# A wait added to GpSimd in the first stage: it stands behind the inverse root until the batch's rows are centred

## The reference, cut to what matters

```
def apply_rope(x):
    x1, x2 = (x[..., :half], x[..., half:])
    return concatenate([x1 * cos - x2 * sin, x1 * sin + x2 * cos], axis=-1)
q = (layernorm(x) @ q_w.T + q_b)   # 16 heads of 16
k = (ctx @ k_w.T + k_b)
v = (ctx @ v_w.T + v_b)
q = apply_rope(q) * d ** (-0.5)
k = apply_rope(k)
```

## Time and profile before

| | |
|---|---|
| median of 3 runs | 4868.27 us (4863.77 to 4871.48) |
| the profiled execution's own time | 4876.46 us |
| its span in the profile | 4874.6 us |
| busy in that span | PE 93%, DVE 74%, ACT 58%, POOL 27% |
| first stage | from 0 to about 264 us of the span |
| mean granted TensorE clock of the span | 0.956 of full speed |

### The profile page before, as it was taken

The page is one execution under the profiler, slowest core; times in us unless marked ns, Lnnn a source line. Parts: engine busy times, 40 slices in busy tenths (PEclk is TensorE's granted clock), DMA queues, the critical chain, the costliest instruction groups (busy, mean ns, idle before and its releaser), DMA issues. The chain is left out here.

```text
span 4874.6 us, 82321 instructions
## 1 busy us (share of the span) xinstructions
PE 4556.2 (93%) x28528; PEld 2715.4 (56%) x28528; DVE 3620.2 (74%) x8718; ACT 2842.8 (58%) x5219; POOL 1331.2 (27%) x940
## 2 busy tenths in 40 slices
PE   8979978997699999999999999999999758999998
PEld 5546646885244444444444444444443547988897
DVE  8978865554468888888888888888886475555554
ACT  4535542223437777777777777777777213444443
POOL 7910002223620110101101101101010224666665
PEclk9989988998879999999999999999998878999999
DMA  6666653223844333343342443333321651333332
GB/s 204 197 170 189 185 154 113 87 70 123 274 94 81 50 69 73 66 82 69 57 76 57 83 80 51 69 74 66 69 49 23 184 162 33 66 83 65 64 66 38
DMA packets 248371, 471.09 MB, mean 97 GB/s; under 512 B 56584, under 2 KB 149384, under 8 KB 247936
## 3 DMA queue, kind: packets, MB, share of 16 engines
q1 hardware_dynamic: 217872, 426.43, 35.6%
q0 software_dynamic: 26720, 38.36, 4.7%
q10 hardware_dynamic: 3360, 0.98, 0.1%
HBM read 240.15 MB, written 144.94 MB: 79 GB/s over the span
## 5 line engine op out<-in xcount | busy, mean ns | idle before, releaser
L1205 DVE TENSOR_REDUCE full_peak<-full_item 128x1 f32<-128x512 f32 (+2 forms) x3392 | 2026.8, 655 | 332.2 <-PE full_item L1267 323.4
L1181 ACT ACTIVATE full_prob<-full_score 128x512 f32<-128x512 f32 (+1 forms) x3328 | 1745.7, 602 | 396.8 <-PE full_score L1277 381.2
L1267 PE MATMUL full_item<-full_kst,full_qst 49*128 49x512 f32 (+1 forms) x4096 | 1170.3, 404 | 8.4 <-DMA full_kst<-full_high 5.6
L1277 PE MATMUL full_score<-full_qst,full_kst 51*128 51x512 f32 (+1 forms) x3328 | 1021.5, 434 | 1.2 <-ACT full_prob L1181 1.2
L1267 PEld LDWEIGHTS full_item<-full_kst,full_qst 49*128 49x128 f32 x4096 | 618.8, 188 | 602.3 <-DVE full_peak L1205 538.1
L1287 PE MATMUL full_value<-full_prob,full_vaug 128*17 128x512 f32 x6656 | 884.5, 603 | 0.6 <-ACT full_prob L1181 0.4
L1277 PEld LDWEIGHTS full_score<-full_qst,full_kst 51*128 51x128 f32 (+1 forms) x3328 | 503.7, 183 | 367.8 <-ACT full_prob L1181 297.7
L1120 POOL TENSOR_TENSOR full_low<-full_low,full_keep 128x1601 f32<-128x1601 f32 x32 | 115.8, 3620 | 1997.9 <-ACT full_low L1155 1997.9
L2505 ACT ACTIVATE moe_h<-moe_hbank,moe_b 128x384 f32<-128x384 f32 (+1 forms) x320 | 199.7, 624 | 442.0 <-PE moe_hbank L2676 401.9
L2686 PE MATMUL moe_ybank<-moe_w_both,moe_h_high 128*128 128x512 f32 x1088 | 386.7, 396 | 0.0
L2539 DVE TENSOR_TENSOR moe_h_low<-moe_h,moe_h_high 128x384 fp32r<-128x384 f32 (+1 forms) x320 | 194.6, 618 | 221.1 <-ACT moe_h_high L2495 208.7
(11 more groups left out here) (299 smaller groups left out, 6796.0 us busy)
## 6 DMA issues: line engine op xcount, KB each, us to landing
full_kst<-full_high SPq DMA_DIRECT2D x256, 200.1 KB
full_ctxT<-in_ctxT SPq DMA_DIRECT2D x16, 1601.0 KB, 8.1
full_kst<-full_low SPq DMA_DIRECT2D x128, 200.1 KB
win_qst<-scratch_q SPq DMA_DIRECT2D x384, 64.0 KB, 2.8
full_qst<-scratch_q SPq DMA_DIRECT2D x384, 64.0 KB
scratch_attn<-win_raw SPq DMA_DIRECT2D x64, 256.0 KB
scratch_q<-open_parts SPq DMA_DIRECT2D x64, 256.0 KB, 3.8
scratch_attn<-full_raw SPq DMA_DIRECT2D x64, 256.0 KB, 2.2
```

Source lines behind the costliest of these rows:

```text
L1181: nc.scalar.activation(prob_of(s, h, kt)[0:rows, :], score[score_bank(u)][0:rows, :], ACT.Exp, scale=SCALE).then_inc(score_read, 1)
L1205: nc.vector.tensor_reduce(peak[s.par][:, hq:hq + len(qts), c], src, AX, ALU.max).then_inc(item_read, 1)
L1267: ins = nc.tensor.matmul(ps[:, at:at + z - a], qst[s.slot][rows, h // 2, qt * P:(qt + 1) * P].bitcast(F32R), kst[s.slot][rows, h // 2, a:z ...
L1277: nc.tensor.matmul(score[score_bank(u)][0:z - a, :], kst[s.slot][rows, h // 2, a:z].bitcast(F32R), qst[s.slot][rows, h // 2, :].bitcast(F3 ...
```

## The change

One line is added to POOL's program. After `power(n + 2)`, where there is one (n from 0 to 13), POOL waits until `xn_done` has counted n + 3, which is when the fourth instruction of `centre(n + 2)` has ended on DVE. Only then does it take the lows of units 2 and 3 of n - 1, the cosines of units 2 and 3 of n, and what follows. No instruction is added, removed or moved on any engine, and no other wait is changed.

More of the change, by code:

```diff
@@ L317, in _ @@
                     power(n + 2)
+                    pool.wait_ge(xn_done, n + 3)
                 if n > 0:
```

## The result

The changed kernel takes 4890.9 us in the median of 6 runs (4887.21 to 4893.76), the kernel before 4868.16 (4857.9 to 4871.48) in the same comparison. The ratio is 1.0041, with a 95% interval of 1.003 to 1.0052: **slower by about 0.4%**, between 15 and 25 us. The forecast was 4884. The medians differ by 22.7 us.

What follows compares the result with a forecast made beforehand. PE, DVE and POOL were taken as all full in the first stage. Terms of -0.8, +15.7 (12 batches at +1.31) and +0.9 gave +15.8 us, 4884.1 on the median; own range +12 to +20, wide range 4872 to 4894.

Steps and rivals of the forecast that it cites:

- steps 1 to 4 of the walk: One batch from centring's end: DVE's row of four to 2.40 us, first low 3.42, turns to 6.66, second add 7.98.
- step 5: Later in that batch: statistics to `values` 2.18 us, rests of units 2 and 3 from 11.96, the first ending at 13.12.
- the price: How far a low on POOL ends behind the DVE instruction that held it up: 1.02 us.
- The first wait that counts: The second wait (the first costs nothing): takes 0.84 us out of centring before its delay is felt, -0.8 us.
- The last term, the delay behind the last wait: Last two batches, which centre nothing: adds up to 1.7 us late, all or none taken up; middle taken, +0.9 us.
- No loss, PE sets the pace: First stage: POOL's delay is absorbed and each batch shrinks by PE's 0.19 us slack, 2.5 us in all; chance 0.10.
- POOL gets in after one instruction: DVE's row of four: POOL takes turns from the start, +2.0 us for each batch, +24.5 in all; chance 0.10.
- A part of it is absorbed: First stage: half the delay finds cover, +0.4 to +0.8 us for each batch, +5 to +10 in all; chance 0.13.
- PE's clock falls: PE idles 1.5 us in each batch and drops to 1.2 GHz, stage up to 170 us longer; chance 0.02.

Runs made afterwards that it cites:

- e3: The changed kernel with a one-column DVE memset between its two rests of units 0 and 1; ratio 1.0049 to the kernel before, batch 17.02 us.
- e4: The changed kernel with the one-column DVE memset behind the second rest instead; ratio 1.0028 to the kernel before, batch 15.96 us.
- e5: The kernel before, without the wait, with a one-column DVE memset behind the second rest; ratio 1.0041 to the kernel before, batch 16.53 us.
- e1: The changed kernel with the same wait placed behind the lows of units 2 and 3; ratio 1.0001 to the kernel before, batch 14.90 us.
- e2: The changed kernel with the wait released by the second of four centring instructions; ratio 1.0098 to the kernel before, batch 18.57 us.
- e7: The changed kernel with POOL's cosine products and lows cut to 4 of 512 columns; ratio 0.9984 to the kernel before, batch 14.63 us.
- e8: The changed kernel with POOL's two cosine products ahead of the two lows behind the wait; ratio 1.0027 to the kernel before, batch 16.08 us.

## Why the prediction was right, point by point

The direction and the mechanism were right; the size, inside the range, was a few microseconds short.

Two sizes have to be kept apart. The stage ends 17.9 us later, inside the forecast's own range of +12 to +20. The medians differ by 22.7 us, above that range; only the wide one, 4872 to 4894, holds 4890.9. Of the 6.8 us between this median and the forecast, the stage explains 2.1. The other 4.7 are in no view: behind the stage the profile of the changed kernel is 0.8 us shorter. The kernel before came to medians of 4868.2, 4870.8, 4872.1 and 4873.5 in the four comparisons, so a median moves by as much, but that this is where the 4.7 come from is not shown.

**The mechanism** held at steps 1 to 4 of the walk, within 0.02 us; step 5 is below. The centrings run undisturbed (1.37 us for four); the first low is kept out until the fourth instruction of DVE's row has ended (146.53, 1.01 behind the sine's end at 145.52; the price was 1.02); the second add starts 8.00 us behind the end of centring (151.11 against 143.11; the walk said 7.98). e3 and e4 show that the keeping out is what a gap in the row decides, and e5 that it was already at work before. e1 shows that the wait has no price of its own.

**The size** was a little too small: 15.8 us forecast, 17.9 measured at the end of the stage. Three terms make it:

- The first wait that counts was to take 0.84 us off; the batch behind it took 16.0 instead of 16.9 us. Right.
- A batch was to be 16.20 us and is 16.27, that is +1.38 instead of +1.31, 0.8 us over twelve batches. Step 5 had two things wrong. The instruction that adds epsilon to the variance (L393) takes 0.93 us instead of 0.42. It reads and writes SBUF, and in both kernels it ends within 0.03 us of the end of POOL's first cosine product, ahead of which it now comes up sooner; beside no work of POOL it takes 0.17 (e2). So the statistics to `values` take 2.69 us where the walk had 2.18. In return the rests of units 2 and 3 come up later, only 0.09 us ahead of the end of POOL's second cosine product, and are no longer held up: 1.28 us for two, where the walk had the first end 1.16 behind its start, 0.48 more. That 0.51 lost and 0.48 regained nearly cancel is luck.
- The last term, the delay behind the last wait, was put at the middle of 0 to 1.7, 0.9. It was 2.2: from the start of the last centring instruction to the end of the stage it is 41.7 us instead of 39.5. On balance the last two batches took up nothing, and added 0.5. This is the term that was mis-sized, and the bound itself was too low. The adds behind the last wait are 1.7 late, as the walk had it. Ahead of the rests of units 0 and 1 of the last batch but one DVE now waits 0.25 us for ACT and not 0.98, which gives 0.7 back. But these rests then take 2.26 us instead of 1.29, since one of them now takes a turn with POOL, and from there on everything is 1.95 late, up to the start of the last partner matmuls. The last 0.27 is PE's clock. Timeline of PE, before and after:

```profile
256.35 3.48 PE L499 MATMUL ctxp_bank<-ctxp_other,ctxp_partner 128*128 128x512 f32 x4 [3.31 <-DVE ctxp_other L413]
273.99 3.75 PE L500 MATMUL ctxp_bank<-ctxp_other,ctxp_partner 128*128 128x512 f32 x4 [3.31 <-DVE ctxp_other L414]
```

In both kernels PE had idled for 3.31 us and the clock had fallen. Its mean over these four matmuls is 0.56 of full speed before and 0.50 with the change: before, it came back from 1.2 to 2.4 GHz at 259.4 us, as the last of them ran, and in the changed kernel all four run at 1.2.

**The rivals.** *No loss, PE sets the pace* fell: the second cosine product ended at 151.00, when DVE had been ready for the second add since 150.56. Its premise, that PE has little slack, was nearly right in size: e7 puts PE's floor at 14.63, 0.26 us below the batch before and not 0.19. *POOL gets in after one instruction* was not what the change does, but e3 makes it happen with a gap of one column, and then it costs what was worked out, 17.02 against 16.9 us. The Trainium skill (SBUF — State Buffer, Who interferes with whom) has whoever issues first hold the shared pair of ports for one whole instruction. The runs agree with it wherever the two engines take turns (sines of 1.64 to 1.75 us in e4). Read as the prediction reads it, that the waiting engine gets in when that one instruction is over, it does not hold for the undisturbed row: three instructions of DVE were let past a waiting one of POOL in each batch. *A part of it is absorbed* is excluded by the stage's end. *PE's clock falls* did not happen in the batches: 1.00 over the stretch, with idle times of 1.41 us. At the end of the stage it falls in both kernels, and there it cost the 0.27 us above.

## What to carry to other kernels

Where two engines take turns as these do, count turns and not overlaps. A stretch of undisturbed, gapless instructions on one of them is worth keeping, and the other's work should fall on instructions that leave the port alone; a wait that moves it from such a place into the row costs more than the collision that it removes (here 0.84 us gained and 2.2 us lost for each batch). Before adding a wait, look at what the released engine meets in the first microsecond after it. And when two engines are full, check how far the third lets them gain: here PE allowed 0.26 us for each batch.

## What the runs showed of the hardware that I had not expected

In these kernels, once a DVE instruction of two SBUF operands has been held up by POOL, DVE no longer keeps POOL out, even if its next instruction is ready: in e4 all four sines behind the gap were held up in turn, at 1.64 to 1.75 us each, and each was issued without a gap behind the one ahead. Undisturbed, the row of two rests and two sines in before and e1 keeps POOL out to its end. So a gap of 0.06 us early in the row is not paid once but for every instruction until one side runs out of work. Why the hardware goes on in either way is open; the runs show only that it does.

POOL's inverse root of four elements is let in behind one instruction: it takes 1.49 us beside DVE's rests and 1.01 where DVE has none of them (e2), it ends 0.86 us behind the end of the rest that it started beside (before, the change and e8 alike), and before and with the change the two rests keep their 1.28 us. That it is small cannot be the whole reason. In e7 the first low of four columns waits for three instructions of DVE, and the next such lows take 0.20 us:

```profile
146.68 1.78 POOL L309 TENSOR_TENSOR ctxp_parts<-ctxp_rest,ctxp_parts 128x4 bf16<-128x4 f32 x1 [4.01 <-DVE ctxp_xn L404]
```

What tells the two apart is open.

The granted clock fell in e3 and e2, whose batches are the longest: to 0.94 and 0.97 of full speed in the mean from 150 to 210 us, which is stretches at 1.2 GHz among those at 2.4. PE did 169 and 162 matmuls in that time, against 175 in the changed kernel. In e3 PE idled for 1.33 and then for 0.57 us in such a batch; in the changed kernel 1.41 us at one piece left the clock alone. So the rival on the clock may have been nearer than its chance of 0.02 says. It cost e3 nothing that shows, since its batches are alike and as long as the walk of DVE and POOL makes them; PE was not what they waited for. Windows of e3, with PE busy, clock and DMA as columns:

```profile
150.00:210.00 60.00, 55.27 (x169) 0.94 0.67 200
```
